# Two up products of the next expert issued half a pair ahead, a state row placed earlier, and the norm's apply and a cast moved from ScalarE to GpSimd

## The chip, the cores and the metric

The kernel runs on one core of a Trainium2 chip. Its time is what the device takes for one execution, in microseconds (us). The engines of the core are TensorE (PE in the profile, its weight loads PEld), VectorE (DVE), ScalarE (ACT), GpSimd (POOL) and SyncE (SP, which here only issues transfers). Each runs its own list of instructions in the order written, and they meet at semaphores.

## What is computed

Two transformer layers over x of shape (1, 2048, 128), each with adaptive layer norms: `h = layernorm(x) * (1 + c) + s`, then `x = x + gate * f(h)`, twice a layer. Layer 0 has a decayed linear attention followed by a small MLP, and then a mixture of experts. Layer 1 has a state-space block and then a Fourier mix with one 128x128 matrix. The change touches the mixture of experts, the state-space block and the norms between them:

```python
# layer 0, second half: 8 experts, hidden width 512, two chosen for each token
probs = softmax(xf @ w_router); topk_w, topk_idx = top_k(probs, 2)
weights = sum(topk_w[..., None] * one_hot(topk_idx, 8), axis=1)
h = gelu(einsum('te,ieh->tih', xf, w1) + b1)
out = sum((einsum('tih,ihe->tie', h, w2) + b2) * weights[..., None], axis=1)
# layer 1, first half: 256 channels, 16 states
x_val = silu(causal_conv4(x @ W_in.T ...)); dt = softplus(x[:, :, :64] @ W_dt.T + b_dt)
Bm = x @ W_B.T; Cm = x @ W_C.T
h = exp(dt_t * A) * h + (dt_t * xv_t) * B_t ; y_t = sum_n h * C_t     # for each token t in turn
y = y * silu(z); out = y @ W_out.T
```

## The kernel before, in words

The 2048 tokens are cut into four chunks c of 512. After the loads, layer 0's attention and the MLP (to about 160 us of the trace) the rest is one long loop over **pairs** p, from -12 to 31, in which every engine walks through `later_stages()` in the same order.

- **Experts.** Pair p also holds expert step g = p + 12, for g from 0 to 31 (8 experts for each of 4 chunks), so pairs -12 to 19. An expert step has four up products `up(g, k)`, each three 128x512 passes on TensorE into one of two banks of `pH` (k even: the first, k odd: the second), then a gelu on ScalarE for each (`hidden`, tile `gel`, which frees the bank), then four down products `down(g, k)` that accumulate into `pO`, and one VectorE step `moe_acc` that adds `pO`, weighted, to `X`. `down(g, 0)` waits for `moe_acc` of the step before.
- **State space.** Pairs 0 to 31 each handle two of the 16 states of a chunk (8 pairs for each chunk). `row_b(m)` is a TensorE matmul that spreads row m of B over the partitions into `pB`, a single bank: it waits until VectorE's `products(m - 1)` has read it. VectorE does `products(m)` (into `pCT`) and two `scans` (`Hs`) for each of the two states, with `moe_acc` between the two. ScalarE makes the factors `dA` one pair ahead (`decays(p + 1)`). GpSimd multiplies by the row of C (`output`, tiles `Acc`, `Zev`, `ZS`) and adds up by transfers until pair 20, TensorE from there (`total`).
- **Stages** are placed in this loop by a table, by the position k = p mod 8: norms (`ln_stats` on VectorE, `ln` on GpSimd for the inverse root, `ln_apply` on ScalarE, `ln_turn`, four transposes on TensorE and a ScalarE activation that empties the bank), routing (`route`, `turn`, `weigh`, `route` in pairs -13, -11, -8 and -5, the other two in the one or two pairs after), and the inputs of the state-space block of the next chunk (`x_part` at k = 5 and 6, `rows` at 5, `dt_part` at 6, `z_part` at 7). A place is a letter: on TensorE A comes before `down(g, 0)`, B between `down(g, 1)` and `down(g, 2)`, C after `down(g, 3)`. On ScalarE the order in a pair is four gelus, four `dA`, then stages A and B, then `apply`, then C.
- **Table loads.** ScalarE loads another function table (ACT_TABLE_LOAD) each time it goes between gelu, exp and silu.

Only two banks hold stages before pair 20: `stage_bank` gives the first for A and C, the second for B.

## Time and profile before

| | us |
|---|---|
| median of 3 runs (lowest, highest) | 607.29 (605.8, 610.0) |
| the profiled execution's own time | 606.43 |
| its span from first to last instruction | 604.4 |
| busy in the span: PE, DVE, ACT, POOL | 482.4, 428.9, 363.4, 313.2 |

The profile is of one execution. Times in a trace are microseconds from the span's start; between the span and the execution's own time lie 2.0 us at the ends. The granted TensorE clock over the span was 0.948 of full speed.

### The profile page before, as it was taken

Reading aid. Unit: us, or ns where it says so; the run is one execution under the profiler, and the core shown is the slowest. Engines: PE = TensorE matmul, PEld = TensorE weight load, DVE = VectorE, ACT = ScalarE, POOL = GpSimd, SP = SyncE. Lnnn points to the kernel's source line nnn. Section 1 sums busy time; section 2 is a strip of 40 time slices with the busy share of each in tenths; the row PEclk is TensorE's granted clock in tenths of the full one; section 3 lists DMA queues with packets and bytes.
Section 4 is the critical chain, followed back from the end, with each engine's and each line's share of the span. In section 5 each row is a group of like instructions: output and inputs, shape, how many; then the busy total and the mean of one; then the engine's idle time right before and its main releaser. Section 6 shows DMA issues by size and latency. Waiting matters only on the chain.

```text
span 604.4 us, 6869 instructions
## 1 busy us (share of the span) xinstructions
PE 482.4 (80%) x2346; PEld 337.7 (56%) x2346; DVE 428.9 (71%) x723; ACT 363.4 (60%) x507; POOL 313.2 (52%) x220
## 2 busy tenths in 40 slices
PE   3869876769899999979869988789897497667573
PEld 3457544434588886757756677657586443233222
DVE  4766798964534334058997779997879985997961
ACT  0531442224664676689999999799988656634201
POOL 3224976866111011314686649767557946566541
PEclk9986999989999999999999989999989779897797
...
GB/s 294 272 1 0 1 1 1 2 0 0 1 0 2 2 1 0 142 1 35 193 147 139 151 139 87 180 136 144 168 75 148 165 20 104 70 63 42 17 0 17
DMA packets 15010, 44.74 MB, mean 74 GB/s; under 512 B 2241, under 2 KB 7745, under 8 KB 12545
## 3 DMA queue, kind: packets, MB, share of 16 engines
...
q14 instruction: 16, 0.12, 0.1%
...
## 4 chain that ended last, share of the span: by engine, by line
PE 24%; ACT 13%; DVE 12%; issue 6%; POOL 3%; DMA 3%; POOLq 0%; ACTq 0%; DVEq 0%
DVE Hs L761 6%; PE pO L1231 5%; DVE pCT L748 4%; ACT dA L985 3%; PE pY L1274 3%; PE pY L1317 3%; ACT gel L973 3%; PE pH L1219 2%; ACT L985 2%; ACT L973 2%; PE pH L1221 2%; PE pH L1220 2%; ACT ln_x L835 2%; PE pH L1274 2%; DMA Acc<-ZS 1%
## 5 line engine op out<-in xcount | busy, mean ns | idle before, releaser
L1231 PEld LDWEIGHTS pO<-w_e,gel 128*128 128x128 f32 x1024 | 124.8, 195 | 14.2 <-issue 8.8
L1231 PE MATMUL pO<-w_e,gel 128*128 128x128 f32 x1024 | 127.2, 279 | 1.4 <-DVE X L732 1.1
L761 DVE TENSOR_TENSOR_SCAN Hs<-dA,HL,pCT 128x512 f32<-128x512 f32 x96 | 117.7, 1268 | 8.1 <-POOL Zev L382 3.8
L382 POOL TENSOR_TENSOR ZS<-Hs,Crow 128x1024 f32<-128x1024 f32 x32 | 76.5, 2392 | 58.3 <-DVE Hs L761 58.3
L973 ACT ACTIVATE gel<-pH,b_e 128x512 f32<-128x512 f32 x128 | 85.9, 687 | 33.3 <-PE pH L1221 32.6
L985 ACT ACTIVATE dA<-dt,a_neg 128x512 f32<-128x512 f32 x128 | 81.9, 710 | 21.0 <-DVE Hs L761 20.7
L748 DVE TENSOR_TENSOR pCT<-u,pB 128x1024 f32<-128x1024 f32 x64 | 78.3, 1224 | 16.7 <-PE pB L1299 15.5
L1219 PE MATMUL pH<-h2h,w_e1h 128*128 128x512 f32 x128 | 57.8, 452 | 22.6 <-ACT gel L973 21.4
L382 POOL TENSOR_TENSOR Zev<-Hs,Crow 128x1024 f32<-128x1024 f32 x26 | 62.8, 2420 | 16.0 <-DVE Hs L761 15.2
L732 DVE SCALAR_TENSOR_TENSOR X<-pO,wts,X 128x128 f32<-128x128 f32 x128 | 35.9, 343 | 43.2 <-PE pO L1231 43.1
L438 POOL TENSOR_TENSOR ZA<-Qsb,S 128x1024 f32<-128x1024 f32 x16 | 38.0, 2374 | 33.6 <-DVE S L656 32.0
L1221 PE MATMUL pH<-h2h,w_e1l 128*128 128x512 f32 x128 | 51.0, 398 | 0.0
L1220 PE MATMUL pH<-h2l,w_e1h 128*128 128x512 f32 x128 | 50.7, 396 | 0.0
L1299 PE MATMUL pB<-ST,sel 96*128 96x512 bf16 x64 | 25.7, 401 | 30.4 <-DVE pCT L748 27.3
L1219 PEld LDWEIGHTS pH<-h2h,w_e1h 128*128 128x128 f32 x128 | 24.1, 188 | 38.6 <-ACT gel L973 34.4
L835 ACT ACTIVATE ln_x<-X,ln_nb,ln_rs 128x128 f32<-128x128 f32 x48 | 19.7, 480 | 36.8 <-POOL ln_nb L354 36.8
L761 DVE TENSOR_TENSOR_SCAN Hs<-dA,pCT 128x512 f32<-128x512 f32 x32 | 37.3, 1207 | 3.8 <-ACT dA L985 2.1
L899 ACT COPY Qsb<-pCT 128x1024 f32<-128x1024 f32 x16 | 16.2, 1013 | 37.2 <-PE pCT L1107 37.2
L1106 PE MATMUL pH<-qk_hi,pick 128*128 128x512 f32 x32 | 16.7, 523 | 23.5 <-DVE S L656 23.5
L973 ACT ACT_TABLE_LOAD x26 | 33.4, 1283 | 0.5
L1299 PEld LDWEIGHTS pB<-ST,sel 96*128 96x128 bf16 x64 | 6.3, 99 | 47.6 <-DVE pCT L748 37.0
L656 DVE TENSOR_TENSOR_SCAN S<-cols,S,pH 128x512 f32<-128x512 f32 x24 | 30.7, 1280 | 0.8
...
## 6 DMA issues: line engine op xcount, KB each, us to landing
...
```

Source lines behind the costliest of these rows:

```text
L382: pool.tensor_tensor(Z, Hs[:, 2 * o:2 * o + 2, 0:w], Crow[:, 2 * (p % NCB) + o:2 * (p % NCB) + o + 1, 0:w].to_broadcast([P, ND, w]), ALU.m ...
L438: pool.tensor_tensor(ZA[:, :, :], Qsb[:, 2 * (R % 2):2 * (R % 2) + 2, :], S[:, 2 * r:2 * r + 2, :], ALU.mult).then_inc(s["att_zo"], 1)
L732: ins = vec.scalar_tensor_tensor(Xj, pO[:, j * P:(j + 1) * P], wts[:, c, j * E + e:j * E + e + 1], Xj, ALU.mult, ALU.add)
L748: vec.tensor_tensor(pU[:, :, 0:w], half_of(u, c), pB[:, None, 0:w].to_broadcast([P, ND, w]), ALU.mult).then_inc(s["mam_ub"], 1)
L761: vec.tensor_tensor_scan(Hs[:, 2 * o + d, 0:w], dA[:, 4 * (p % 2) + 2 * o + d, 0:w], pU[:, d, 0:w], HL[:, d, n:n + 1] if c else 0.0, ALU.m ...
L973: nc.scalar.activation(gel[:, n % NG, 0:w], pH[n % 2][:, 0:w], ACT.Gelu_apprx_tanh, bias=b_e1[:, NK * e + k:NK * e + k + 1]).then_inc(s["m ...
L985: nc.scalar.activation(dA[:, 4 * (p % 2) + r, 0:WIDTHS[c]], half_of(dt, c)[:, r % 2, :], ACT.Exp, scale=a_neg[:, r % 2, n:n + 1]).then_inc ...
L1219: mm(pH[n % 2][:, 0:w], w_e1h[:, g % E, part], h2h[:, c, 0:w], start=True, stop=False)
L1220: mm(pH[n % 2][:, 0:w], w_e1h[:, g % E, part], h2l[:, c, 0:w], start=False, stop=False)
L1221: mm(pH[n % 2][:, 0:w], w_e1l[:, g % E, part], h2h[:, c, 0:w], start=False, stop=True).then_inc(s["moe_h"], 1)
L1231: ins = mm(pO[:, j * P:(j + 1) * P], gel[:, n % NG, j * P:(j + 1) * P], w_e2[:, NK * (g % E) + k, :], start=(k == 0 and j == 0), stop=(k = ...
L1299: mm(pB[:, 0:w], sel[:, n:n + 1].to_broadcast([96, P]), ST[:, c % 2, 0:w], start=True, stop=True).then_inc(s["mam_bB"], 1)
```

## The change

Four things are edited. `ln_apply` leaves ScalarE: GpSimd's `ln` now subtracts the mean and multiplies by the inverse root itself, four `tensor_scalar` of 128x128, and no longer makes the negative mean and the bias (`ln_nm`, `ln_nb`). The cast of the B and C rows to bf16 (`ST`) goes from ScalarE to GpSimd's `rows`. A new place U lies between the first two and the last two up products of a pair (on ScalarE between the gelus of the first two and of the last two); the `ln_turn` of the next chunk's state-space input goes there, from C at k = 4 to U at k = 5, and uses the second stage bank. And `up(g + 1, 0)` and `up(g + 1, 1)` are issued in pair p, behind `down(g, 1)` and ahead of place B, where they stood at the start of pair p + 1; `row_b(2p + 2)` goes from behind `down(g, 1)` to behind `down(g, 0)` in the pairs that have no stage at A.

```diff
-            return (2 if p < ALONE else 0) + int(at == "B")
+            return (2 if p < ALONE else 0) + int(at in ("B", "U"))
...
-                             (2, "end", "ln_stats", tail), (3, "apply", "ln_apply", tail), (3, "C", "ln_turn", tail, 2),
+                             (2, "end", "ln_stats", tail), (3, "C", "ln_turn", tail, 2),
                              (3, "end", "bias", tail), (4, "B", "fft", tail)]
                 if 0 <= front < NL:
-                    plan += [(4, "mid", "ln_stats", front), (4, "apply", "ln_apply", front), (4, "C", "ln_turn", front, 1),
+                    plan += [(4, "mid", "ln_stats", front), (5, "U", "ln_turn", front, 1),
                              (5, "A", "x_part", front, 0), (5, "B", "rows", front), (6, "A", "x_part", front, 1),
                              (6, "B", "dt_part", front, 0), (6, "C", "dt_part", front, 1), (7, "mid", "step", front),
                              (7, "A", "z_part", front, 0), (7, "B", "z_part", front, 1)]
                 for q in range(1, NL):
                     at = k - (p + AHEAD - 3 * (q - 1))
-                    plan += [(at, "mid", "ln_stats", q), (at, "apply", "ln_apply", q), (at + 1, "A", "ln_turn", q, 0),
+                    plan += [(at, "mid", "ln_stats", q), (at + 1, "A", "ln_turn", q, 0),
                              (at + 1, "B", "route", q), (at + 2, "A", "turn", q), (at + 2, "B", "weigh", q)]
...
                 pool.wait_ge(s["ln_stats"], L[0] + 1)
-                pool.wait_ge(s["ln_xn"], L[0])
-                pool.tensor_scalar(ln_nm[:, 0:J], ln_mv[:, 0:J, 0], -1.0, None, ALU.mult)
                 link(pool.tensor_scalar(ln_ve[:, 0:J], ln_mv[:, 0:J, 1], EPS, None, ALU.add))
                 link(pool.tensor_tensor(ln_rs[:, 0:J], ln_ve[:, 0:J], mhalf[:, 0:J], ALU.pow))
-                pool.tensor_tensor(ln_nb[:, 0:J], ln_nm[:, 0:J], ln_rs[:, 0:J], ALU.mult).then_inc(s["ln_rstd"], 1)
+                pool.wait_ge(s["ln_tr"], L[0])
+                for j in range(J):
+                    ins = pool.tensor_scalar(ln_x[:, j, :], rows_of(X, c)[:, j, :], ln_mv[:, j, 0:1], ln_rs[:, j:j + 1],
+                                             ALU.subtract, ALU.mult)
+                ins.then_inc(s["ln_xn"], 1)
...
-                pool.wait_ge(s["mam_st0"], c + 1)
-                pool.wait_ge(s["ln_rstd"], L[0])
+                pool.wait_ge(s["mam_bcs"], c + 1)
+                pool.wait_ge(s["ln_xn"], L[0])
                 for name, count in done.items():
                     if count:
                         pool.wait_ge(s[name], count)
+                link(pool.tensor_copy(st, bc))
...
-            def ln_apply(c):
-
-                act.wait_ge(s["ln_rstd"], A[0] + 1)
-                act.wait_ge(s["ln_tr"], A[0])
-                for j in range(blocks(c)):
-                    ins = nc.scalar.activation(ln_x[:, j, :], rows_of(X, c)[:, j, :], ACT.Identity,
-                                               bias=ln_nb[:, j:j + 1], scale=ln_rs[:, j:j + 1])
-                ins.then_inc(s["ln_xn"], 1)
-                A[0] += 1
...
                 nc.scalar.copy(BCf[:, c % 2, 0:w], PS[b][0:96, 0:w]).then_inc(s["mam_bcs"], 1)
-                act.wait_ge(s["mam_bcs"], c + 1)
-                nc.scalar.copy(ST[:, c % 2, 0:w], BCf[:, c % 2, 0:w]).then_inc(s["mam_st0"], 1)
...
             for p, stages in later_stages():
                 if 0 <= p + AHEAD < NL * E:
-                    hidden(p + AHEAD, range(NK))
+                    hidden(p + AHEAD, (0, 1))
+                run(p, stages, "U")
+                if 0 <= p + AHEAD < NL * E:
+                    hidden(p + AHEAD, (2, 3))
                 if 0 <= p + 1 < NL * NP:
                     decays(p + 1)
                 run(p, stages, "AB")
-                run(p, stages, ("apply",))
                 run(p, stages, "C")
...
                 g = p + AHEAD
                 moe = 0 <= g < NL * E
-                if moe:
-                    up(g, 0)
-                    up(g, 1)
+                if any(at == "U" for at, *_ in stages) and not moe:
+                    run(p, stages, "U")
                 if 0 <= p < NL * NP:
                     row_b(2 * p + 1)
+                if moe:
+                    run(p, stages, "U")
                 if moe:
                     up(g, 2)
                     up(g, 3)
@@ -1254,9 +1242,13 @@
                     total(p - 1)
                 if moe:
                     down(g, 0)
-                    down(g, 1)
                 if not early and 0 <= 2 * p + 2 < NL * NS:
                     row_b(2 * p + 2)
+                if moe:
+                    down(g, 1)
+                if g + 1 < NL * E:
+                    up(g + 1, 0)
+                    up(g + 1, 1)
                 run(p, stages, "B")
                 if moe:
                     down(g, 2)
```

TensorE, the opening (route of chunk 0, then expert step 0), before (L1196 route, L1219 to L1221 an up product, L1231 down products, L1202 `turn`):

```order
L1196 MATMUL pY<-w_router,h2T 128x8 x4
L1219 MATMUL pH<-h2h,w_e1h 128x512
L1220 MATMUL pH<-h2l,w_e1h 128x512
L1221 MATMUL pH<-h2h,w_e1l 128x512
L1219 MATMUL pH<-h2h,w_e1h 128x512
L1220 MATMUL pH<-h2l,w_e1h 128x512
L1221 MATMUL pH<-h2h,w_e1l 128x512
L1219 MATMUL pH<-h2h,w_e1h 128x512
```

and after (there L1183 is the route, L1206 to L1208 an up product):

```order
L1206 MATMUL pH<-h2h,w_e1h 128x512
L1207 MATMUL pH<-h2l,w_e1h 128x512
L1208 MATMUL pH<-h2h,w_e1l 128x512
L1206 MATMUL pH<-h2h,w_e1h 128x512
L1207 MATMUL pH<-h2l,w_e1h 128x512
L1208 MATMUL pH<-h2h,w_e1l 128x512
L1183 MATMUL pY<-w_router,h2T 128x8 x4
L1206 MATMUL pH<-h2h,w_e1h 128x512
```

The route stood ahead of all up products and stands behind two of them now.

TensorE, the end of a pair at k = 6, before (L1274 `x_part`, L1285 `dt_part`):

```order
L1274 MATMUL pY<-h3T,w_cx 128x512 x4
L1231 MATMUL pO<-w_e,gel 128x128 x8
L1285 MATMUL pY<-h3T,w_dt 128x512
L1231 MATMUL pO<-w_e,gel 128x128 x8
L1285 MATMUL pY<-h3T,w_dt 128x512
```

and after (L1266 `x_part`, L1218 down products, L1277 `dt_part`):

```order
L1266 MATMUL pY<-h3T,w_cx 128x512 x4
L1218 MATMUL pO<-w_e,gel 128x128 x8
L1206 MATMUL pH<-h2h,w_e1h 128x512
L1207 MATMUL pH<-h2l,w_e1h 128x512
L1208 MATMUL pH<-h2h,w_e1l 128x512
L1206 MATMUL pH<-h2h,w_e1h 128x512
L1207 MATMUL pH<-h2l,w_e1h 128x512
L1208 MATMUL pH<-h2h,w_e1l 128x512
L1277 MATMUL pY<-h3T,w_dt 128x512
L1218 MATMUL pO<-w_e,gel 128x128 x8
L1277 MATMUL pY<-h3T,w_dt 128x512
```

Both `dt_part` now stand behind two up products of the next step.

ScalarE, pairs 4 and 5, before (L985 `dA`, L835 `ln_apply`, L849 the emptying of the bank, L973 gelu, L940 `x_part`, L950 and L952 `rows`):

```order
L985 ACTIVATE dA<-dt,a_neg 128x512 x4
L835 ACTIVATE ln_x<-X,ln_nb,ln_rs 128x128 x4
L849 ACTIVATE h3T<-pY,mods 128x512
L973 ACT_TABLE_LOAD
L973 ACTIVATE gel<-pH,b_e 128x512 x4
L985 ACT_TABLE_LOAD
L985 ACTIVATE dA<-dt,a_neg 128x512 x4
L940 ACT_TABLE_LOAD
L940 ACTIVATE xc<-pY,cols 128x512
L950 COPY BCf<-pY 96x512
L952 CAST ST<-BCf 96x512
```

and after (L972 `dA`, L960 gelu, L839 the emptying):

```order
L972 ACTIVATE dA<-dt,a_neg 128x512 x4
L960 ACT_TABLE_LOAD
L960 ACTIVATE gel<-pH,b_e 128x512 x2
L839 ACTIVATE h3T<-pY,mods 128x512
L960 ACTIVATE gel<-pH,b_e 128x512 x2
L972 ACT_TABLE_LOAD
L972 ACTIVATE dA<-dt,a_neg 128x512 x4
L929 ACT_TABLE_LOAD
L929 ACTIVATE xc<-pY,cols 128x512
L939 COPY BCf<-pY 96x512
```

The apply and the cast are gone from ScalarE, and the emptying stands between the gelus of the next pair.

## Rows read from the trace of the kernel before

**Rows 1.** Windows: stretch, length, busy PE, PEld, DVE, ACT, POOL, clock, DMA share, GB/s

```profile
164.00:272.00 108.00, 101.79 (x635) 81.81 (x633) 39.72 (x130) 71.94 (x107) 17.61 (x24) 1.00 0.06 21
272.00:352.00 80.00, 68.63 (x398) 53.05 (x398) 69.57 (x106) 74.45 (x99) 50.80 (x31) 1.00 0.58 138
```

**Rows 2.** Timeline, the opening: start, us, engine, line, operation, tiles, idle before it

```profile
159.14 0.49 PEld L1029 LDWEIGHTS pH<-ident,ln_x 128*128 128x128 f32 x4 [0.53 <-ACT ln_x L835]
...
161.41 1.06 PE L1196 MATMUL pY<-w_router,h2T 128*128 128x8 f32 x8
...
162.82 0.50 PE L1219 MATMUL pH<-h2h,w_e1h 128*128 128x512 f32 x1 [0.35 <-POOL h2l L466]
...
162.96 0.23 ACT L929 ACTIVATE ex<-lg 128x32 f32<-128x32 f32 x1 [0.30 <-DVE lg L705]
...
163.62 0.40 PE L1219 MATMUL pH<-h2h,w_e1h 128*128 128x512 f32 x1
...
164.50 1.27 ACT L973 ACTIVATE gel<-pH,b_e 128x512 f32<-128x512 f32 x2
...
165.24 0.50 PE L1219 MATMUL pH<-h2h,w_e1h 128*128 128x512 f32 x1 [0.76 <-ACT gel L973]
```

**Rows 3.** Timeline of ACT, expert step 1

```profile
171.44 1.26 ACT L973 ACTIVATE gel<-pH,b_e 128x512 f32<-128x512 f32 x2
```

**Rows 4.** Timeline of ACT, the route of chunk 2 in pair -8

```profile
202.37 0.23 ACT L929 ACTIVATE ex<-lg 128x32 f32<-128x32 f32 x1 [0.37 <-DVE lg L705]
...
204.43 1.39 ACT L973 ACTIVATE gel<-pH,b_e 128x512 f32<-128x512 f32 x2 [0.54 <-PE pH L1221]
```

**Rows 5.** Timeline of DVE, `moe_acc` of a pair without stages

```profile
188.88 1.12 DVE L732 SCALAR_TENSOR_TENSOR X<-pO,wts,X 128x128 f32<-128x128 f32 x4 [1.10 <-PE pO L1231]
```

**Rows 6.** Timeline, ACT and PE in pair 2, which has no stage

```profile
288.10 1.27 ACT L973 ACTIVATE gel<-pH,b_e 128x512 f32<-128x512 f32 x2
...
288.84 0.50 PE L1219 MATMUL pH<-h2h,w_e1h 128*128 128x512 f32 x1 [1.22 <-ACT gel L973]
...
291.23 1.28 ACT L985 ACT_TABLE_LOAD   x1
...
292.52 2.57 ACT L985 ACTIVATE dA<-dt,a_neg 128x512 f32<-128x512 f32 x4
```

**Rows 7.** Timeline, ACT and DVE around pair 5

```profile
314.05 0.78 ACT L849 ACTIVATE h3T<-pY,mods 128x512 f32<-128x512 f32 x1 [0.81 <-PE pY L1029]
...
316.27 1.23 DVE L748 TENSOR_TENSOR pCT<-u,pB 128x1024 f32<-128x1024 f32 x1
...
325.03 0.57 ACT L950 COPY BCf<-pY 96x512 f32<-96x512 f32 x1
```

**Rows 8.** Chain that ended last, pair 5: start, us, engine, tile, line, count

```profile
318.77 3.44 PE pY L1274 x8
322.20 1.78 PE pO L1231 x16
```

**Rows 9.** Timeline of ACT, the second `dt_part` of pair 6

```profile
338.95 0.69 ACT L959 ACTIVATE dt<-pY,cols 128x512 f32<-128x512 f32 x1 [0.32 <-PE pY L1285]
```

**Rows 10.** Timeline, PE in pair 8 and DVE in pair 9

```profile
353.95 3.53 PE L1231 MATMUL pO<-w_e,gel 128*128 128x128 f32 x16
...
357.73 1.23 DVE L748 TENSOR_TENSOR pCT<-u,pB 128x1024 f32<-128x1024 f32 x1 [3.19 <-PE pB L1299]
```

**Rows 11.** Timeline, PE in pair 10 and ACT in pair 11

```profile
372.78 0.39 PE L1299 MATMUL pB<-ST,sel 96*128 96x512 bf16 x1 [1.83 <-DVE pCT L748]
...
379.27 1.39 ACT L973 ACTIVATE gel<-pH,b_e 128x512 f32<-128x512 f32 x2 [2.42 <-PE pH L1221]
```

**Rows 12.** Timeline of ACT, the last `ln_apply`

```profile
595.11 1.65 ACT L835 ACTIVATE ln_x<-X,ln_nb,ln_rs 128x128 f32<-128x128 f32 x4 [24.62 <-POOL ln_nb L354]
```

**Rows 13.** Groups of POOL by line and shape: count, busy us, mean ns, idle us

```profile
L352 POOL TENSOR_SCALAR ln_ve<-ln_mv 128x4 f32<-128x4 f32 x12 | 2.7, 226 | 0.8
...
L450 POOL TENSOR_TENSOR w_out<-w_out,gates 128x256 f32<-128x256 f32 x1 | 0.7, 729 | 0.0
```

More of the change, by code:

```diff
@@ L87, in build @@
         ln_rs = sb("ln_rs", [P, NJ])
-        ln_nm = sb("ln_nm", [P, NJ])
-        ln_nb = sb("ln_nb", [P, NJ])
         ln_x = sb("ln_x", [P, NJ, D])
@@ L242, in build @@
             mam_hist mam_xp mam_zp mam_gz mam_dtp mam_bc mam_bcs mam_xc mam_dt mam_u
-            mam_st0 mam_st mam_cd mam_bB mam_ub mam_dA mam_sc mam_z mam_zs  mam_y mam_y2 mam_o mam_x
+            mam_st mam_cd mam_bB mam_ub mam_dA mam_sc mam_z mam_zs  mam_y mam_y2 mam_o mam_x
             fft_o fft_b fft_x vec_chain act_chain pool_chain out_done""".split()
@@ L283, in later_stages @@
             for stage in (("A", "total", NL * NP - 1), ("end", "gate", last), ("A", "project", last), ("end", "tail_x", last),
-                          ("end", "bias", last), ("mid", "ln_stats", last), ("apply", "ln_apply", last),
+                          ("end", "bias", last), ("mid", "ln_stats", last),
                           ("A", "ln_turn", last, 2), ("A", "fft", last)):
@@ L534, in ln_stats @@
                 Xc = rows_of(X, c)
-                vec.wait_ge(s["ln_rstd"], L[0])
+                vec.wait_ge(s["ln_xn"], L[0])
                 L[0] += 1
@@ L815, in _ @@
             L = [0]
-            A = [NC]
             def link(ins):
@@ L923, in _ @@
                 if c == 3:
-                    ln_apply(0)
                     ln(h2T[:, 0:WIDTHS[0]], 0, 2, 1, h2h[:, 0, 0:WIDTHS[0]])
@@ L996, in run @@
                         continue
-                    if stage == "ln_apply":
-                        ln_apply(c)
-                    elif stage in ("ln_turn", "route", "turn", "x_part", "rows", "dt_part", "z_part"):
+                    if stage in ("ln_turn", "route", "turn", "x_part", "rows", "dt_part", "z_part"):
                         {"ln_turn": turned, "route": route, "turn": turn, "x_part": x_part, "rows": rows, "dt_part": dt_part,
```

## The prediction, before the changed kernel was run

> **What bounds the kernel now.** I read the windows first, then the timelines of single pairs, then the chain. The windows split the loop. From 164 to 272 us (pairs -12 to -1) TensorE is busy 101.8 of 108 us and ScalarE 71.9; from 272 to 352 (pairs 0 to 7) ScalarE has 74.5 of 80, TensorE 68.6, VectorE 69.6 [rows 1]. So the first stretch is TensorE's. The reader should see in [rows 6] that a mixed pair without a stage is a closed ScalarE loop: two gelus 1.27, 0.47 until the third product is there, two gelus 1.39, a table load 1.28, four `dA` 2.57, a load, in all 8.3. TensorE there waits 1.22 for a gelu, so it is not the bound. VectorE needs two products of 1.23, four scans, `moe_acc` 1.12 [rows 5]: about 8.5, later 8.8 with the states carried over. It lags a little behind ScalarE in each such pair, and makes it good in the pairs with stages, where ScalarE takes 11 to 13. After pair 19 VectorE sets the end. Three engines within half a microsecond of each other mean that what one gives up is soon taken by the next.
>
> **What does not change in a mixed pair.** Two up products ahead do not remove ScalarE's 0.47: the third product needs the bank that the first gelu empties, and starts 0.74 after that gelu's start (288.10 to 288.84) [rows 6], whether or not the first two lay ready. Those pairs stay at 8.3.
>
> **First stretch: the new order puts two up products ahead of things ScalarE waits for.** Two up products take about 1.40 (one starts 0.80 after the other, cold from a wait; after that 0.7 each) [rows 2]. Two down products take 1.78, the 8 passes of an `x_part` 3.44 [rows 8].
>
> Opening. The first `ln_apply` leaves ScalarE too, which was still at the MLP: TensorE waited 0.53 for its `ln_x` [rows 2]. GpSimd is idle there, so the apply is early enough and all after it comes 0.5 sooner. The route was issued at 161.41 and its exp ran at 162.96, 1.55 later; the first gelu at 164.50, 1.54 after that, the third product at 165.24 [rows 2]. Now two up products precede the route, and they wait for GpSimd's `h2l`, at 162.82 less 0.5. Route 162.3 + 1.4 = 163.7, exp 165.3, gelu 166.8, third product 167.5: 2.3 later. Then `turn` (place C) is copied by ScalarE ahead of the gelus of step 1. The pair runs 167.5 + 1.40 + 1.78 + 1.40 + 1.78 = 173.9, and with the copy and its waits (0.5) the gelu starts at 174.4 against 171.44 [rows 3]: **3.0 later**.
>
> Route pairs. In pair -8 exp ran at 202.37, the next gelu at 204.43, 0.54 of it waiting for TensorE [rows 4]. The route comes 1.40 later, exp at 203.75, load 1.28, gelu 205.3, third product 206.0 where it was 205.2. VectorE's ranking ends 3.5 after exp, then `moe_acc` 1.12, then `down(g, 0)`: 208.4, was 207.06. What comes back: in a pair without a stage TensorE no longer waits the 0.35 for the gelus, but only two up products (1.40) now lie between `down(g, 3)` and the next `down(g, 0)`, while `moe_acc` needs 1.5 from the last down product (0.38 to its start, 1.12) [rows 5], so 0.2 of each 0.35 to 0.4 stays. Net for a route pair and the two behind it: +0.7 (pairs -11 to -9), +0.8 (-8 to -6), +0.5 (-5 and -4, where the transposes that moved to U spare a wait of 0.5). With the opening 3.0 + 2.0 = 5.0.
>
> Inputs of chunk 0. In pair -3 `rows` comes 1.40 later on TensorE and ScalarE waits for it: +0.65, as the cast's 0.62 is spared. In pair -2 the second `dt_part` is at C, behind all; ScalarE follows it at once (in pair 6 it waited 0.32 [rows 9]), then load, gelu, third product. It is 1.40 later and nothing of it is hidden: +1.35. **Sum of the first stretch: 5.0 + 2.0 = +7.0 us**, at 272.
>
> **Mixed stretch.** Pair 4 loses `ln_apply` (1.65 [rows 12]), the wait 0.81 and the emptying 0.78 [rows 7] on ScalarE: -3.1 (11.4 to 8.3). Pair 5 gives it back: `row_b(12)` stands ahead of `x_part` and waits for the product of VectorE that starts at 316.27 [rows 7]. VectorE is not moved, so TensorE stands until 317.5: x_part 317.8 to 321.2, two downs to 323.0, two ups to 324.4, `rows` to 325.3, copy (before at 325.03 [rows 7]) 325.5 to 326.05, load, gelu 327.35 against 327.56. Net -0.2. Pair 6 has the late `dt_part` again: +1.6. So pairs 0 to 7 take 1.4 longer in all.
>
> In pair 8 VectorE waited 3.19 for `row_b(18)` [rows 10]. It now comes one down product earlier, but the scans also need the `dA` that ScalarE makes 5.7 after the pair's first gelu, in place just before the scans start, so the gain is 0.2 only. Pair 10: `row_b(22)` waits 1.83 for VectorE, and the gelu of pair 11 then 2.42 [rows 11]. The gelu comes earlier, but TensorE behind that wait has the same products to do in all, and the third product is where it was. Pairs 11 and 12: ScalarE is free of two applies and a turn; in 11 it then waits for the transposes at C (-0.5), in 12 it gains the 3.1. Pair 13 starts at 398.55, was 402.15: -5.0 since pair 8. Pairs 13 and 14 as 5 and 6, with `row_b(28)` waiting: +4.3. Counted from the start of pair 0, expert steps so reach pair 16 0.7 late (1.4 - 5.0 + 4.3). From there VectorE sets the end, and it was held by `row_b(34)` as by `row_b(18)` in [rows 10]. That row now comes a down product earlier, the factors `dA` of pair 17 (made after the gelus of 16) become the last thing, and the scans that began at 445.04 begin at 444.15 on the same count: **-0.9 for the stretch**.
>
> **GpSimd's prices.** A `tensor_scalar` of 128x128 is not in the trace: between 0.23 (the four-column one, L352) and 0.73 (two inputs, 256 columns, L450) [rows 13]; I take 0.45, four make 1.8. The wait for GpSimd is covered in pair 5 (ready about 312.5, wanted 313.5); at 2.9 it would cost 0.6 there and in 13. The cast, between 0.23 and 1.46 (twice L450), is covered: row 0 of the chunk is wanted 10 us later. The last norm is on the path: four of 0.45 with 0.2 between them replace 1.65 of ScalarE [rows 12], and two small steps (0.23 and 0.20) go: -0.3; between -1.0 and +0.8. The same at pair 21: -0.3. **Tail -0.6.** The Trainium skill, "GPSIMD Engine Reference", section "Elementwise — side-by-side cycle accounting", has one tensor input at some 1.03 cycles for each element; by that a `tensor_scalar` would be an estimated 0.35 and the tail -1.0. No run here shows it yet.
>
> **The clock.** The new order leaves TensorE idle for about 2.9 us at four places: the opening, and pairs -2, 6 and 14, from the last `dt_part` until the third product. The granted clock fell behind idle time in this trace: the 16 down products before `row_b(18)` took 3.53, where 16 took 1.78 elsewhere [rows 8, 10], and that is the larger part of the 3.19. A fall costs about 1.4 in such a place (two up products at half speed, with a gelu behind each). I take one more than before: **+1.4**. The Trainium skill, "TensorE: Matmul & The Clock Gate", section "The HAM clock gate", says that the clock follows how busy the array has lately been; by that all four are in danger, a rival below.
>
> **Sum.** +7.0 - 0.9 - 0.6 + 1.4 = +6.9. The profiled execution took 606.43, so 613.3; it lies 0.86 under the median of the runs. Between the two scales I say **613.8**.
>
> **Rivals.**
> 1. ScalarE's saving is kept (the other side). If VectorE is not in the way in pairs 5 and 13, ScalarE's sums hold: -2.9 in each of pairs 4 and 12 with the emptying put between the gelus, -1.5 in 11, -1.2 for two casts, -8.5. And if the first stretch gets the whole 0.35 back in nine pairs (-3.1) and the route pairs cost nothing, it is 3.0 - 3.1 + 2.0 = +1.9. With the tail: 606.4 - 8.5 + 1.9 - 0.6 = 599.2. It decides if `row_b` in pair 5 finds its product done. For it: the busy sums in [rows 1]. Against: the start at 316.27 [rows 7], which nothing in the change moves ahead.
> 2. No difference. Opening and `dt_part` cost as said, but block 1's 5.0 survives because pairs 13 and 14 cost half (2.1), and the route pairs cost nothing: 7.0 - 2.0 - 0.9 - 2.2 - 0.6 = +1.3, 607.7. For it: ranking and `moe_acc` have slack elsewhere.
> 3. The clock falls at all four places: 606.4 + 5.5 (the sum without the 1.4) + 5.6 = 617.5. For it: idle of 1.9 to 2.2 was enough before pair 8 and before pair 16. Against: the same idle before pair 0 was not, and no such fall is seen at the opening.
>
> **Chances.** Forecast 0.42, rival 1 0.18, rival 2 0.28, rival 3 0.12. The range reaches from just above rival 1 to just over rival 3: 602 to 619; the bounds of GpSimd's prices (-0.7 to +2.3) lie in it. A change of 1% (6.1 us) is about what a measurement of this kernel tells from none. 613.4 is that edge, and my forecast stands just beyond it, so a part of its own case falls within: slower 0.48, same 0.33, faster 0.19.
>
> **What would show it.** Right: the first route's exp near 165.3, the first gelu of step 1 near 174.4, pair 0 starting 7 us late; `L1291` at pair 5 waiting some 2 us for VectorE; a ScalarE wait before the `dt` of pairs -2, 6 and 14. Wrong: a first stretch of 108 us or less, or pairs 5 and 13 at 11 us after an 8.3; also a `tensor_scalar` above 1 us, or scans waiting for GpSimd.

## The result: 3.3% slower, outside the range

The changed kernel takes 626.32 us (median of 4 runs, 625.82 to 627.58) against 606.84 before: a ratio of 1.0327, 95% interval 1.0293 to 1.0361. The forecast was 613.8, range 602 to 619. The profiled execution took 625.94, with a span of 623.2 and a mean granted clock of 0.93 (before 606.43, 604.4 and 0.948).

The same two windows as in [rows 1], now of the changed kernel:

```profile
164.00:272.00 108.00, 95.21 (x591) 79.83 (x590) 34.35 (x125) 56.71 (x80) 26.71 (x32) 0.97 0.06 20
272.00:352.00 80.00, 68.98 (x394) 53.39 (x392) 64.79 (x100) 69.18 (x90) 50.87 (x32) 0.97 0.50 117
```

TensorE, the bound of the first stretch, did 95.2 us of work there where it did 101.8, and the granted clock is no longer 1.00 throughout.

The opening, timeline of PE and ACT, answers to [rows 2] and [rows 3]:

```profile
161.83 0.50 PE L1206 MATMUL pH<-h2h,w_e1h 128*128 128x512 f32 x1 [1.33 <-POOL h2l L466]
...
163.33 0.96 PE L1183 MATMUL pY<-w_router,h2T 128*128 128x8 f32 x8
...
164.78 0.23 ACT L918 ACTIVATE ex<-lg 128x32 f32<-128x32 f32 x1 [3.12 <-DVE lg L706]
...
166.32 1.26 ACT L960 ACTIVATE gel<-pH,b_e 128x512 f32<-128x512 f32 x2
...
167.06 0.79 PE L1206 MATMUL pH<-h2h,w_e1h 128*128 128x512 f32 x1 [2.77 <-ACT gel L960]
167.65 0.63 PE L1207 MATMUL pH<-h2l,w_e1h 128*128 128x512 f32 x1
...
175.52 1.27 ACT L960 ACTIVATE gel<-pH,b_e 128x512 f32<-128x512 f32 x2
```

The route's exp runs 1.45 behind the route (163.33 to 164.78; before 1.55); the route itself stands behind two up products; and the third product (L1206 at 167.06) had TensorE idle for 2.77 us. Behind that, the passes take 0.63 instead of 0.39: the granted clock has fallen. Windows of the same run around that place, the 8 passes of `x_part` in pair 5 and the start of pair 7:

```profile
166.00:170.00 4.00, 2.94 (x8) 2.36 (x9) 3.25 (x14) 2.26 (x4) 0.33 (x2) 0.63 0.00 0
326.80:332.00 5.20, 5.12 (x9) 2.34 (x10) 5.09 (x7) 3.92 (x6) 3.72 (x2) 0.67 0.87 176
354.00:357.00 3.00, 3.00 (x8) 2.01 (x9) 2.93 (x5) 1.86 (x3) 0.04 (x1) 0.62 0.49 101
```

Pair 5, timeline, answers to [rows 7] and [rows 8]:

```profile
325.59 1.23 DVE L749 TENSOR_TENSOR pCT<-u,pB 128x1024 f32<-128x1024 f32 x1
...
326.88 0.39 PE L1291 MATMUL pB<-ST,sel 96*128 96x512 bf16 x1 [2.02 <-DVE pCT L749]
...
327.10 3.29 PE L1266 MATMUL pY<-h3T,w_cx 128*128 128x512 f32 x4
...
329.33 3.07 PE L1266 MATMUL pY<-h3T,w_cx 128*128 128x512 f32 x5
...
336.47 0.58 ACT L939 COPY BCf<-pY 96x512 f32<-96x512 f32 x1 [3.35 <-PE pY L1272]
...
338.37 1.26 ACT L960 ACTIVATE gel<-pH,b_e 128x512 f32<-128x512 f32 x2
```

`row_b(12)` (L1291) waits 2.02 for VectorE's product, as forecast. `x_part` then lasts from 327.10 to 332.23, 5.1 us instead of 3.44. The second `dt_part` of pair 6 and the first product behind it, answer to [rows 9]:

```profile
351.25 0.69 ACT L946 ACTIVATE dt<-pY,cols 128x512 f32<-128x512 f32 x1 [1.81 <-PE pY L1277]
...
353.99 0.50 PE L1206 MATMUL pH<-h2h,w_e1h 128*128 128x512 f32 x1 [2.56 <-ACT gel L960]
```

GpSimd, the group of the apply by line and shape (count, busy us, mean ns, idle us), and, from the timeline, an apply with the products queued behind it, two scans of VectorE, the transposes of pair 21 and those of the last norm, answer to [rows 12] and [rows 13]:

```profile
L352 POOL TENSOR_SCALAR ln_x<-X,ln_mv,ln_rs 128x128 f32<-128x128 f32 x48 | 37.5, 792 | 1.3
```

```profile
394.84 3.12 POOL L352 TENSOR_SCALAR ln_x<-X,ln_mv,ln_rs 128x128 f32<-128x128 f32 x4
397.94 4.65 POOL L382 TENSOR_TENSOR ZS<-Hs,Crow 128x1024 f32<-128x1024 f32 x2
...
400.42 2.45 DVE L762 TENSOR_TENSOR_SCAN Hs<-dA,HL,pCT 128x512 f32<-128x512 f32 x2 [1.70 <-POOL ZS L382]
...
489.24 1.28 DVE L762 TENSOR_TENSOR_SCAN Hs<-dA,HL,pCT 128x512 f32<-128x512 f32 x1 [1.78 <-POOL ZS L382]
...
500.99 1.08 PE L1016 MATMUL pH<-ident,ln_x 128*128 128x128 f32 x4 [3.26 <-POOL ln_x L352]
...
612.29 3.13 POOL L352 TENSOR_SCALAR ln_x<-X,ln_mv,ln_rs 128x128 f32<-128x128 f32 x4
...
615.56 1.09 PE L1016 MATMUL pH<-ident,ln_x 128*128 128x128 f32 x4 [6.87 <-POOL ln_x L352]
```

One `tensor_scalar` takes 0.79, not 0.45. VectorE waits for GpSimd's `ZS` 1.70 and 1.78 at two places where it did not wait before: the products `ZS` start at 397.94, when the apply ahead of them in GpSimd's list is through. In pair 21 TensorE waits 3.26 for `ln_x` itself; before it waited 1.93 for ScalarE's, as this row of the timeline before shows:

```profile
483.73 1.08 PE L1029 MATMUL pH<-ident,ln_x 128*128 128x128 f32 x4 [1.93 <-ACT ln_x L835]
```

### The profile page after: what moved, and what is told of

It reads as the page before. It is cut to its first block, busy times and chain, and to the rows that moved or that the text cites. A ratio compares the mean times of both kernels' runs of the same rounds, so it can differ in the third digit from the quotient of the medians.

```text
span 623.2 us, 6833 instructions
## 1 busy us (share of the span) xinstructions
PE 488.3 (78%) x2346; PEld 345.3 (55%) x2346; DVE 428.1 (69%) x723; ACT 340.9 (55%) x455; POOL 347.9 (56%) x248
## 4 chain that ended last, share of the span: by engine, by line
PE 38%; DVE 31%; ACT 14%; POOL 7%; issue 6%; DMA 3%; ACTq 0%; POOLq 0%; DVEq 0%
DVE Hs L762 8%; PE pO L1218 8%; DVE pCT L749 5%; DVE S L657 5%; PE pH L1206 4%; PE pY L1266 4%; PE pH L1208 3%; PE pH L1207 3%; PE pY L1309 3%; ACT L960 3%; DVE pH L656 3%; ACT gel L960 3%; ACT dA L972 2%; ACT L972 2%; POOL ZS L382 2%
## 5 line engine op out<-in xcount | busy, mean ns | idle before, releaser
L1218 PEld LDWEIGHTS pO<-w_e,gel 128*128 128x128 f32 x1024 | 125.7, 193 | 18.3 <-issue 9.8
L1218 PE MATMUL pO<-w_e,gel 128*128 128x128 f32 x1024 | 128.0, 276 | 3.0 <-DVE X L733 3.0
L960 ACT ACTIVATE gel<-pH,b_e 128x512 f32<-128x512 f32 x128 | 85.0, 686 | 40.4 <-PE pH L1208 39.8
L972 ACT ACTIVATE dA<-dt,a_neg 128x512 f32<-128x512 f32 x128 | 81.9, 711 | 21.0 <-DVE Hs L762 20.7
L749 DVE TENSOR_TENSOR pCT<-u,pB 128x1024 f32<-128x1024 f32 x64 | 78.3, 1224 | 10.4 <-PE pB L1291 9.3
L1206 PE MATMUL pH<-h2h,w_e1h 128*128 128x512 f32 x128 | 58.5, 457 | 34.4 <-ACT gel L960 33.0
L1291 PE MATMUL pB<-ST,sel 96*128 96x512 bf16 x64 | 26.3, 411 | 37.5 <-DVE pCT L749 34.3
L1208 PE MATMUL pH<-h2h,w_e1l 128*128 128x512 f32 x128 | 52.6, 411 | 0.0
L1207 PE MATMUL pH<-h2l,w_e1h 128*128 128x512 f32 x128 | 52.2, 408 | 0.0
L1206 PEld LDWEIGHTS pH<-h2h,w_e1h 128*128 128x128 f32 x128 | 24.9, 194 | 46.5 <-ACT gel L960 41.8
L352 POOL TENSOR_SCALAR ln_x<-X,ln_mv,ln_rs 128x128 f32<-128x128 f32 x48 | 37.5, 792 | 1.3
L1291 PEld LDWEIGHTS pB<-ST,sel 96*128 96x128 bf16 x64 | 6.5, 101 | 51.6 <-DVE pCT L749 45.5
L382 POOL TENSOR_TENSOR Acc<-Hs,Crow 128x1024 f32<-128x1024 f32 x6 | 14.2, 2368 | 36.1 <-DVE Hs L762 36.1
```

The costliest lines, as they stand in the source:

```text
L352: ins = pool.tensor_scalar(ln_x[:, j, :], rows_of(X, c)[:, j, :], ln_mv[:, j, 0:1], ln_rs[:, j:j + 1], ALU.subtract, ALU.mult)
L382: pool.tensor_tensor(Z, Hs[:, 2 * o:2 * o + 2, 0:w], Crow[:, 2 * (p % NCB) + o:2 * (p % NCB) + o + 1, 0:w].to_broadcast([P, ND, w]), ALU.m ...
L749: vec.tensor_tensor(pU[:, :, 0:w], half_of(u, c), pB[:, None, 0:w].to_broadcast([P, ND, w]), ALU.mult).then_inc(s["mam_ub"], 1)
L960: nc.scalar.activation(gel[:, n % NG, 0:w], pH[n % 2][:, 0:w], ACT.Gelu_apprx_tanh, bias=b_e1[:, NK * e + k:NK * e + k + 1]).then_inc(s["m ...
L972: nc.scalar.activation(dA[:, 4 * (p % 2) + r, 0:WIDTHS[c]], half_of(dt, c)[:, r % 2, :], ACT.Exp, scale=a_neg[:, r % 2, n:n + 1]).then_inc ...
L1206: mm(pH[n % 2][:, 0:w], w_e1h[:, g % E, part], h2h[:, c, 0:w], start=True, stop=False)
```

## Where the time goes, place by place

The part of the program ahead of the experts, which the change hardly touches, differs by up to 2.9 us between single executions: ScalarE's last activation of the MLP began at 156.87 before and between 155.72 and 158.57 in the others of the table. So I compare places with that difference taken off. The table gives the start of VectorE's product for row m of the profiled run, less that of before, less the difference at that activation. m = 0 is the start of pair 0, 12 to 17 are pairs 6 and 7 with the inputs of chunk 1, 17 and 18 stand on either side of the wait in [rows 10], 25 and 41 follow the two new waits for `ZS`, 44 follows the transposes of pair 21, 25 to 33 hold the inputs of chunk 2, 34 is where VectorE takes over, 63 is the last. The last column is the median of the runs.

```
run          m=0    12    17    18    24    25    33    34    40    41    44    63  median
changed     10.6  10.3  15.8  12.5  12.5  14.2  18.4  15.2  15.2  16.9  18.6  18.8   626.3
ups         13.7  13.9  19.7  17.2  17.4  17.4  22.4  20.0  20.1  20.2  19.6  19.6   630.7
a_nogp      12.7  13.0  17.4  14.1  14.1  14.1  20.6  17.3  17.8  17.8  17.2  17.2   624.4
a_behind     1.1   2.0   5.8   2.5   2.5   4.4   9.2   5.9   6.4   7.9   9.2   9.3   617.4
a_noups     -0.4   0.7   0.0  -2.8  -1.7   0.1  -1.5  -4.0  -2.9  -1.2   0.2   0.2   609.4
a_quiet     -1.0  -0.1  -1.0  -3.5  -2.5  -0.5  -2.0  -4.5  -3.5  -1.7   0.0   0.6   607.8
a_noups_tt  -1.1  -0.5  -1.5  -4.0  -2.9  -2.4  -2.2  -4.7  -3.7  -3.2  -3.2  -3.3   604.7
gp           0.9   2.3   1.8   0.2   0.4   2.0   2.0   2.0   2.0   3.7   5.4   5.6   611.5
row          0.0   0.0   0.1  -1.3  -1.3  -1.3  -1.3  -3.7  -2.7  -2.7  -3.2  -3.3   604.2
rt          -0.5   0.3  -0.6  -3.1  -2.1  -2.1  -3.5  -4.6  -4.5  -4.5  -5.6  -4.8   601.1
rtc         -0.4   0.3  -0.6  -3.1  -2.1  -2.1  -3.5  -4.8  -4.8  -4.8  -5.8  -6.1   601.6
rtc_quiet   -1.7  -1.6  -2.6  -5.1  -4.1  -4.1  -5.6  -7.0  -6.2  -6.2  -7.6  -7.7   599.4
a_warm      10.9  10.9  17.1  13.8  14.6  16.2  22.9  19.6  20.4  22.4  23.4  23.2   630.3
a_warm2      7.6   8.6  10.8   9.0   9.2  11.1  13.7  12.0  12.4  14.2  15.7  15.8   623.7
a_warm5      9.2  10.2  12.3  10.5  11.0  12.8  15.5  12.2  13.2  16.2  17.3  17.3   624.9
```

Between two places where one row of the table does not move, the kernel runs at the old pace. A row is one execution of its kernel: `a_warm2` and `a_warm5` lie 1.6 apart at m = 0, and up to there their instructions are the same, so a difference of that size between two rows is not yet an effect of the edit.

## The experiments

The first four split the change in two: the order of the up products, and GpSimd.

**The up products alone (`ups`).**

```diff
 # before.py, in pair()
-                if moe:
-                    up(g, 0)
-                    up(g, 1)
...
+                if g + 1 < NL * E:
+                    up(g + 1, 0)
+                    up(g + 1, 1)
                 run(p, stages, "B")
```

> The kernel before, with one part of the change alone: up(g+1, 0) and up(g+1, 1) behind down(g, 1) and ahead of place B. Theory 1 (order: the two up products stand ahead of route, rows and dt_part, for which ScalarE waits, and the granted clock falls behind the idle time that this makes): pair 0 starts 8 to 9 us late, pairs 6 and 14 take 1.5 more each with a slow TensorE behind them, in all +11 to +14, about 619. Theory 2 (GpSimd: its tensor_scalar at 0.79 us, nearly twice what was forecast, makes most of the loss): this part alone costs no more than the 7 forecast for the first stretch, 611 to 613.

Measured: 630.7 (627.4 to 631.9), ratio 1.0394 (1.0333 to 1.0454). More than either theory: 13.7 late at pair 0, another 6 by m = 17. This part alone is no faster than the whole change, since the other parts of the change give some of it back, as the runs below show.

**GpSimd alone (`gp`).** The edits of the change to `ln`, `rows`, `ln_apply` and the table's "apply" entries; `ln_turn` stays at C of k = 4.

> The kernel before, with the norms' apply and the cast on GpSimd alone; every place as before. Theory 1 (order): GpSimd's share is what the trace of the changed kernel shows at four places where VectorE or the chain waits for it, 1.7 + 1.7 + 1.7 + 1.0, less about 0.3 in each of pairs 4 and 12 on ScalarE: +4 to +6, about 611.5. Theory 2 (GpSimd is the larger part): +10 or more, above 616. Theory 3 (the savings on ScalarE count when TensorE's order is left alone): at or under 606.

Measured: 611.5 (609.0 to 615.3), ratio 1.0082 (1.0048 to 1.0116). Theory 1. The table shows three steps: +1.6 between m = 24 and 25, +1.7 between 40 and 41, +1.7 between 41 and 44.

**The change without its up products (`a_noups`) and without GpSimd (`a_nogp`).** The diffs are the two above taken back from the changed kernel.

> The changed kernel with all four up products of a step back at the start of its pair (as before); norms and cast on GpSimd, turn at U, earlier row_b stay. Theory 1: the loss of the first stretch is gone (pair 0 starts within 1 us of 271.5) and GpSimd's 4 to 6 stay: 609 to 613. Theory 2: most of the loss stays, 616 or more.

> The changed kernel with the norms' apply and the cast back on ScalarE. Theory 1: the 9 us of the first stretch stay, the waits of VectorE for ZS near 400 and 489 and the longer last norm go: 618 to 621, and pair 4 takes about 10 us instead of 8.3. Theory 2: 613 or less.

Measured: 609.4 (ratio 1.0035, 1.0007 to 1.0063) and 624.4 (1.0283, 1.0228 to 1.0338). So the up products ahead, with what they do to the clock, cost 17 us (626.3 to 609.4), and GpSimd's part costs 1.9 in their presence against 5.0 by itself. `a_noups` is theory 1. `a_nogp` took 3 us more than theory 1 gave. It is 2.1 later than the changed kernel at pair 0, most of that (1.6) already in the first expert step, at a granted clock of 0.73 from 164 to 175 where the changed kernel had 0.84 (more on this under the clock, below); and it gets it back from m = 24 on, where it has no wait for `ZS`.

The next four ask where the up products cost, and what the other two parts do.

**Up products behind place B (`a_behind`).**

```diff
 # after.py, in pair()
-                if g + 1 < NL * E:
-                    up(g + 1, 0)
-                    up(g + 1, 1)
                 run(p, stages, "B")
+                if g + 1 < NL * E:
+                    up(g + 1, 0)
+                    up(g + 1, 1)
```

> The changed kernel with the two up products behind place B instead of ahead of it; all else as changed. Theory 1 (they cost where they stand ahead of route, rows and dt_part): the opening and the route pairs are as before, only the second dt_part and turn, at C, are still behind them: of the 17 us between the changed kernel and the one without up products ahead 3 to 7 are left, 612 to 617. Theory 2 (two up products ahead cost by themselves, wherever they stand in the pair, by the down products that they put off): over 620.

**Up products ahead only in pairs with nothing at B or C (`a_quiet`).**

```diff
+            busy = {p for p, stages in later_stages() if any(at in ("B", "C") for at, *_ in stages)}
...
-                if g + 1 < NL * E:
+                if g + 1 < NL * E and -AHEAD <= p and p not in busy:
                     up(g + 1, 0)
                     up(g + 1, 1)
```

> The changed kernel with the two up products ahead only in pairs that have no stage at B or C (pairs without route, weigh, rows, dt_part, z_part or turn there). Theory 1: none of the 17 us is left, 606 to 610. Theory 2: since these are two thirds of the pairs, more than a third of the 17 stays, 615 or more.

Measured: 617.4 (ratio 1.0176, 1.0123 to 1.0229), at the edge of what theory 1 gave, and 607.8 (1.0008, 0.9973 to 1.0044), theory 1. Moved behind B, the products leave pair 0 only 1.1 late instead of 10.6; what is left is the second `dt_part` at C (+3.8 from m = 12 to 17, +4.8 from 25 to 33) and GpSimd. Kept out of pairs with a stage at B or C, they cost nothing that shows (607.8 against 609.4 without any). Two up products ahead are harmless by themselves; ahead of a stage that ScalarE waits for, they cost.

**The row alone (`row`), row and turn (`rt`), row, turn and cast (`rtc`).** `row` is the hunk that moves `row_b(2p + 2)` up by one down product; `rt` adds place U; `rtc` adds the cast on GpSimd.

> The kernel before, with row_b(2p + 2) behind down(g, 0) rather than down(g, 1) alone. Theory 1: VectorE's waits for row_b(18) and row_b(34), 3.2 us each, shrink to what the factors dA allow, with half of the 16 slow down products no longer ahead of it: -1 to -4, 603 to 606. Theory 2 (as forecast, dA decides 0.2 later): no difference.

> The kernel before with row_b earlier and ln_turn at U; norms and cast stay on ScalarE. Theory 1 (turn at U between the gelus is what brings the 2.6 us between the version with row_b alone, 604.2, and that with turn and cast as well, 601.6): 601 to 603. Theory 2 (the cast on GpSimd brings it): 604.

> The kernel before with row_b earlier, ln_turn at U and the cast on GpSimd; the norms' apply stays on ScalarE and the up products stay at the start of their pair. Theory 1 (the four tensor_scalar of 0.79 make VectorE wait for GpSimd near 400 and 489 and lengthen the last norm, in all 4 to 6): this runs 2 to 5 us under the version with the apply on GpSimd (609.4) and under the kernel before, 602 to 606. Theory 2 (the apply on ScalarE costs as much as it costs on GpSimd): 608 to 611.

Measured: 604.2 (ratio 0.9953, 0.9920 to 0.9986), 601.1 (0.9923, 0.9904 to 0.9941) and 601.6 (0.9909, 0.9877 to 0.9941). The row is a gain, theory 1: small, with an interval that just excludes 1. The turn comes out as 3.1 more by the medians and 1.8 by the ratios, whose intervals overlap; the table has it too (-1.3 against -3.5 at m = 33). The cast on GpSimd makes no difference that shows. `rtc` and `a_noups` differ in nothing but the engine of the apply: 601.6 against 609.4, 7.8 us where theory 1 gave 2 to 5. With the row and the turn in place the apply on GpSimd costs more than the 5.0 of `gp`. The pair behind [rows 10], timeline of `row`:

```profile
353.88 1.91 PE L1231 MATMUL pO<-w_e,gel 128*128 128x128 f32 x8
...
355.58 0.63 PE L1300 MATMUL pB<-ST,sel 96*128 96x512 bf16 x1
...
356.12 2.56 ACT L985 ACTIVATE dA<-dt,a_neg 128x512 f32<-128x512 f32 x4
...
356.25 1.23 DVE L748 TENSOR_TENSOR pCT<-u,pB 128x1024 f32<-128x1024 f32 x1 [1.83 <-PE pB L1300]
357.54 2.45 DVE L761 TENSOR_TENSOR_SCAN Hs<-dA,HL,pCT 128x512 f32<-128x512 f32 x2
```

TensorE issues the row behind 8 slow down products instead of 16, VectorE's wait is 1.83 instead of 3.19, and the scans begin right behind the product, 1.42 after the first `dA`, and not behind all four (356.12 + 2.56).

**The fastest, with the idea of the change added where it is harmless (`rtc_quiet`).** `rtc` and the diff of `a_quiet`.

> The fastest version so far (row_b earlier, turn at U, cast on GpSimd, apply on ScalarE, 601.6) and two up products ahead in the pairs without a stage at B or C. Theory 1: as in the version with the apply on GpSimd, where this gave -1.6 within its spread, the gain of 0.2 in a few pairs is the most: 600.5 to 602. Theory 2 (the idea has a gain of its own once GpSimd is out of the way): under 599.

Measured: 599.4 (597.8 to 600.5), ratio 0.9898 (0.9867 to 0.9929): the fastest of all, faster than both kernels. It lies between the two theories. Against `rtc` it is 2.2 by the medians, 1.6 by the last column but one and 0.7 by the ratios; with the spread of `rtc` (596.8 to 603.4) a gain of its own isn't settled.

**The clock (`a_warm`, `a_warm2`, `a_warm5`).** Products on TensorE that nobody reads, in the gaps.

```diff
 # after.py, end of pair(); five in a_warm, two in a_warm2 and a_warm5
                 run(p, stages, "C")
+                if p in (-AHEAD - 1, -2, 6, 14):
+                    if g >= 0:
+                        pe.wait_ge(s["moe_acc"], g + 1)
+                    for _ in range(2):
+                        mm(pO[:, 0:TC], w_in[:, 0, :], X[:, 0:NJ, :], start=True, stop=True, skip_group_check=True)
 # a_warm5 also, ahead of the early row_b
+                if p in (5, 13):
+                    pe.wait_ge(s["moe_acc"], g)
+                    mm(pO[:, 0:TC], w_in[:, 0, :], X[:, 0:NJ, :], start=True, stop=True, skip_group_check=True)
```

> The changed kernel with five idle products of 128x512 added on TensorE (their result is overwritten unread) at four places: behind the first route, and at the end of pairs -2, 6 and 14, where it stood still for 2.6 to 2.8 us and the granted clock then fell to 0.6 to 0.7. Theory 1 (the clock follows this idle time, and each fall costs 0.7 to 1.6 us): the clock stays at 1.0 behind all four, and the time falls by 3 to 4 us, 622 to 623.5. Theory 2 (the fall comes from something else, or is hidden): 626 as the changed kernel.

Measured: 630.3 (ratio 1.0404, 1.0374 to 1.0433), slower. Each product is two passes of 0.43, so five took 4.3 us and overran the gap, as this row of its timeline shows:

```profile
354.18 4.56 PE L1264 MATMUL pO<-X,w_in 128*128 128x512 f32 x10 [0.36 <-DVE X L735]
```

The clock stayed at 1.00 behind all four, but the run gives no price for it. So two products:

> As the run with five idle products, but with two (1.7 us by the 0.43 for each of their two passes that it showed, within the 2.6 to 2.8 for which TensorE stood still). Theory 1 (the slow passes behind the four idle places cost 0.7 to 1.6 us each, and five products only ran on past the gap): clock 1.0 behind them, 621 to 624. Theory 2 (the fall is hidden behind ScalarE and VectorE and costs nothing): 625.5 to 627.5.

> The same with one more idle product ahead of row_b(12) and row_b(28) in pairs 5 and 13, where TensorE waits 2.0 and 2.75 us for VectorE's product; the 8 passes of x_part behind the first took 5.1 us at a clock of 0.65. Theory 1: x_part takes 3.4 in both, and up to 1.7 us less in pair 5 than in the run with two products alone, 620 to 622.5. Theory 2: the pair's length is set elsewhere, same as that run.

Measured: 623.7 (ratio 1.0299, 1.0265 to 1.0333) and 624.9 (1.0307, 1.0275 to 1.0340). The windows of `a_warm2` at the three places shown above:

```profile
168.00:171.00 3.00, 2.19 (x13) 1.93 (x14) 2.79 (x11) 2.51 (x5) 0.00 (x0) 1.00 0.00 0
326.80:332.00 5.20, 5.09 (x22) 3.17 (x23) 5.10 (x7) 4.65 (x7) 3.44 (x2) 1.00 0.77 154
352.00:356.00 4.00, 3.78 (x20) 2.69 (x20) 3.69 (x5) 3.50 (x5) 0.09 (x1) 1.00 0.44 90
```

The clock is 1.00 in all three. The time is 2.6 lower than that of the changed kernel by the medians, 3.0 by the table (18.8 to 15.8) and 1.7 by the ratios, whose intervals overlap; `a_warm5` is 1.4, 1.5 and 1.2 lower. So what two products give back is some 1 to 3 us of the 17. It is not the whole price of the clock: windows of a third of a pair with a clock of 0.85 or less lie in six places of the changed kernel (the opening and pairs -1, 5, 7, 12 and 15), in two of the kernel before (pairs 8 and 16) and of `a_noups` (the opening and pair 0), and still in four of `a_warm2` (pairs 0, 8, 12 and 16). How the remaining 14 to 16 us divide between the order and those falls, no run here shows.

The price of single falls does show. In pair 5 the clock of `a_warm2` stayed up although nothing was added there and TensorE had been idle for 2.01 us. From `row_b(12)` to the first gelu of pair 6 it takes 9.80 (326.91 to 336.71), the changed kernel 11.49 (326.88 to 338.37): the slow `x_part` costs 1.7, all of it on the path. The product that `a_warm5` adds in that place had nothing to save.

The distance of `a_warm5` to `a_warm2` has a cause in the trace as well. Its clock fell in the opening ahead of the added products, behind the wait for `h2l`:

```profile
163.85 0.79 PE L1209 MATMUL pH<-h2h,w_e1h 128*128 128x512 f32 x1 [1.34 <-POOL h2l L468]
164.44 0.63 PE L1210 MATMUL pH<-h2l,w_e1h 128*128 128x512 f32 x1
```

`a_nogp` does the same behind 1.33 us, and this is its 1.6 in the first expert step; the changed kernel and `a_warm2` waited 1.33 and 1.34 there and ran on at full clock.

**GpSimd's prices (`prices`).** Eight instructions in the opening, on a tile that nobody reads:

```diff
 # before.py, GpSimd's route(0)
+                    for o, i in ((scr[:, 0, :], ident[:, :]), (scr[:, :, :], wide)):
+                        link(pool.tensor_scalar(o, i, one, two, ALU.subtract, ALU.mult))
+                        link(pool.tensor_scalar(o, i, one, None, ALU.subtract))
+                        link(pool.tensor_scalar(o, i, 2.0, None, ALU.mult))
+                        link(pool.tensor_tensor(o, i, i, ALU.subtract))
```

> The kernel before with eight more instructions on GpSimd in the opening, on a tile that nobody reads: for 128x128 and for 128x512 each a tensor_scalar with two columns as operands (subtract, mult), one with one column, one with one constant, and a tensor_tensor. Their durations count, not the time. If the second operation costs: 0.79 for the first of 128x128 and about 0.45 for the next two. If it is a fixed price for each instruction: 128x512 takes well under four times as long. If it is the two operands: the first stands alone at 0.79 and 3.1.

The timeline of POOL:

```profile
167.73 0.81 POOL L474 TENSOR_SCALAR scr<-ident,cols 128x128 f32<-128x128 f32 x1
168.65 0.66 POOL L475 TENSOR_SCALAR scr<-ident,cols 128x128 f32<-128x128 f32 x1
169.39 0.80 POOL L476 TENSOR_SCALAR scr<-ident 128x128 f32<-128x128 f32 x1
170.28 0.45 POOL L477 TENSOR_TENSOR scr<-ident 128x128 f32<-128x128 f32 x1
170.83 2.14 POOL L474 TENSOR_SCALAR scr<-ident,cols 128x512 f32<-128x512 f32 x1
173.07 1.56 POOL L475 TENSOR_SCALAR scr<-ident,cols 128x512 f32<-128x512 f32 x1
174.72 1.49 POOL L476 TENSOR_SCALAR scr<-ident 128x512 f32<-128x512 f32 x1
176.29 1.04 POOL L477 TENSOR_TENSOR scr<-ident 128x512 f32<-128x512 f32 x1
```

Neither the second operation alone (0.81 against 0.66 and 0.80 for 128x128) nor the operands explain 0.8: four times the columns cost 2.14 / 0.81 = 2.6 times as much. Nearly half of a 128x128 is a fixed part: from the two sizes, (2.14 - 0.81) / 384 = 3.5 ns a column and 0.37 fixed. A `tensor_tensor` of 512 columns takes 1.04.

**The apply as two `tensor_tensor` of 512 columns (`a_noups_tt`).**

```diff
 # a_noups, GpSimd's ln()
-                for j in range(J):
-                    ins = pool.tensor_scalar(ln_x[:, j, :], rows_of(X, c)[:, j, :], ln_mv[:, j, 0:1], ln_rs[:, j:j + 1], ...)
+                link(pool.tensor_tensor(ln_x[:, 0:J, :], rows_of(X, c), ln_mv[:, 0:J, 0:1].to_broadcast([P, J, D]), ALU.subtract))
+                ins = pool.tensor_tensor(ln_x[:, 0:J, :], ln_x[:, 0:J, :], ln_rs[:, 0:J, None].to_broadcast([P, J, D]), ALU.mult)
```

> The changed kernel without up products ahead (609.4), and with the norm's apply on GpSimd as two tensor_tensor over all 512 columns (mean and inverse root broadcast) instead of four tensor_scalar of 128x128. By the prices measured, two of 1.04 to 1.3 for 3.14. Theory 1 (what GpSimd takes for the apply passes straight into the waits of VectorE near 387 and 475 and into the last norm): 0.5 to 1 less in each of four places, 606 to 608. Theory 2 (the cost is the order of GpSimd's queue, not the duration): 609 to 610.

Measured: 604.7 (ratio 0.9972, 0.9946 to 0.9998), below theory 1. The two instructions and the waits for `ZS`, timeline:

```profile
392.17 1.04 POOL L353 TENSOR_TENSOR ln_x<-X,ln_mv 128x512 f32<-128x512 f32 x1
393.29 1.04 POOL L355 TENSOR_TENSOR ln_x<-ln_x,ln_rs 128x512 f32<-128x512 f32 x1
...
383.73 2.45 DVE L765 TENSOR_TENSOR_SCAN Hs<-dA,HL,pCT 128x512 f32<-128x512 f32 x2 [0.58 <-POOL ZS L385]
...
468.98 1.28 DVE L765 TENSOR_TENSOR_SCAN Hs<-dA,HL,pCT 128x512 f32<-128x512 f32 x1 [0.56 <-POOL ZS L385]
```

2.16 from start to end for 3.14 (the waits go from 1.86 and 1.78 in `a_noups` to 0.58 and 0.56). So the duration counts, and theory 2 falls; another place in GpSimd's queue was not tried. The apply on ScalarE (`rtc`, 601.6) stays 3 us faster.

## Why the prediction was wrong

**Direction and main mechanism were right, two terms were not.** Slower, by the up products ahead of what ScalarE waits for: that came as forecast. The steps that failed are GpSimd's cover (put at nothing in the loop and -0.6 at the norms, +6.1 measured) and, behind it, the clock (one fall more than before, four measured). The rival of the other side (savings kept, 599.2) and "no difference" fell; the third, the clock falling at all four places (617.5), describes what the trace shows, and its size was still short.

**First stretch, +7.0.** Measured 10.6 at m = 0. `a_warm2`, which kept the clock at 1.00 through this stretch, is at 7.6, and it agrees term by term. By the third gelu of the pairs it is 3.6 late at pair -11 (the opening), 5.5 at -3 (route pairs +1.9, forecast 2.0), 6.2 at -2 (`rows` +0.7, forecast 0.65) and 7.6 at -1 (`dt_part` +1.4, forecast 1.35). Two steps in the opening were off. The "0.5 sooner" did not come: TensorE was still at the MLP's last product, and the 0.53 belonged to its weight load; aligned, the transposes started where they had. And the slow passes cost 1.6 by the gelu of step 1 (175.52 + 1.01 - 171.44 = 5.1 late, where the same sum without a fall and without the 0.5 gives 3.5). The rest of the 3.0 between 10.6 and 7.6 comes with the fall in pair -1.

**Pairs 4 to 6.** Pair 4 -3.1 and pair 6 +1.5 came as forecast (-3.1, +1.6). Pair 5 took 4.6 more, not 2.9: the wait for VectorE was as forecast, and `x_part` behind it ran 1.7 longer at a clock of 0.67. I had listed four idle places for the clock and not this one.

**The clock, +1.4.** I took one more fall than before, 1.4. There were four more: six places against two, among them all four of rival 3. The two that the traces price by themselves cost 1.6 (the opening) and 1.7 (pair 5); what all of them cost together stays open, with the 1.2 to 3.0 that `a_warm2` and `a_warm5` gave back as a part of it.

**GpSimd's prices.** This is the step that failed most. The value taken, 0.45, and the upper bound, 0.73 from two inputs of 256 columns in [rows 13], both lie under the 0.79 measured. Worse, the cover was checked only in pairs 5 and 13. "The wait for GpSimd is covered" looked at who needs `ln_x`; it did not look at what is queued behind the apply on GpSimd itself. There it is `output`, the products `ZS`, and VectorE's scans need the buffer that they free: two steps of 1.7, between m = 24 and 25 and between 40 and 41, forecast as nothing. In pair 21 the transposes wait for `ln_x` itself, another 1.7 between 41 and 44 for the -0.3 forecast, and the last norm gives +1.0 (18.8 at m = 63, 19.8 at the end) for the other -0.3. Together about 6.7 of the 13 that the forecast missed. (Taking the apply back to ScalarE saved only 1.9 in `a_nogp`, since ScalarE then pays for it; in `rtc` it saved 7.8.) The Trainium skill's "GPSIMD Engine Reference", section "Elementwise — side-by-side cycle accounting", whose figure gave the estimate of 0.35, is further off still for this shape: the page names the dispatch of an instruction as a cost without a figure, and here the fixed part (0.37) and the part by columns (0.44) are each as large as that whole estimate. The tail of -1.0 beside it was added up wrongly, too: counted as the -0.3 was, 0.35 gives some -1.4 over the two norms.

**Pairs 8 to 12, -5.0, and the row.** They gave -3.6 by the first gelus (14.0 late at pair 8, 10.4 at 13) and -3.0 by the third (14.0 and 11.0). The items that the forecast names there, -0.5 and -3.1, add up to 3.6 as well; it gives none for the other 1.4. From m = 18 to 24 no run of the table gains on the kernel before, whatever its ScalarE has saved; I read this as VectorE's pace. The row was undersold: "the gain is 0.2 only", since the scans would wait for four `dA`. They wait for the first two, and the row alone gave 1.4 and 2.4 at the two places; in the changed kernel the same places give 3.3 and 3.2 (15.8 to 12.5, 18.4 to 15.2). That gain hides a part of the forecast's other misses.
